# A graph network in three edge passes: how far GpSimd may gather ahead of the sums

## The chip, the cores and the metric

One NeuronCore of a Trainium2 chip runs the kernel, with its five engines: TensorE (PE in the profile, PEld for its weight loads), VectorE (DVE), ScalarE (ACT), GpSimd (POOL) and SyncE (SP). The metric is the time of one execution on the device in microseconds (us), as the median of several runs.

## The reference

A graph of 6250 nodes with 128 features and 100000 edges, sorted by destination, so each node's incoming edges stand in a row. Two layers work on it, each added to its input and normalised over the features:

```
x = layernorm(x + sigmoid(gcn(relu(gcn(x, W1, b1)), W2, b2)))      # both gcn over the same edges
x = layernorm(x + attention(x, edge_attr, fc_w, fc_r_w, attn_w, loop_w))

gcn(x, W, b)    h = x W;  out[d] = sum over edges (s, d) of h[s] * dinv[s] * w * dinv[d], plus b
                dinv = 1/sqrt(sum of the edge weights into a node, and 1 for its own loop)
attention       z = x fc_w^T;  r = edge_attr fc_r_w^T
                e = leakyrelu(z[s].a0 + z[d].a1 + r.a2);  alpha = softmax of e over the edges into d
                out[d] = relu(sum of alpha * (z[s] + r), plus z loop_w)
```

## The kernel before, in words

**Tiles and groups.** Edges go by tiles of 128 (T = 782), tiles by groups of eight (G = 98). For each tile the kernel needs the feature rows of its 128 source nodes. GpSimd fetches them with one indirect DMA for a tile (L720), at an offset column of `srcC`, into a slot of `ring` in SBUF. VectorE makes for each tile a 128 x 128 matrix S (`build_S`, L1608), which holds an edge's weight at the column of its destination within a window, and TensorE multiplies the gathered rows by S into a PSUM bank that collects the window's nodes (`sum_group`, L858). A node bank is closed when its last group is in: ScalarE copies it out, TensorE applies the layer's weights, and so on.

**Three passes.** Pass 0 and pass 1 are the two gcn layers, pass 2 is the attention. A pass begins its gathers when the table it reads (`x1_d`, `h1_d`, `x2_d`) has been written whole. Nine sets of 32 tiles need no gather in some passes: their rows come from a node table in SBUF by one-hot matmuls (`look_up`, L898, with one-hots that ScalarE makes at L1239 and L1241) and are summed in slots (`make_slots`, L1681 on VectorE; `sum_slots`, L910 on TensorE). In pass 0 six sets are so made, in pass 1 all nine, in pass 2 three (`XR`). So the gathered groups are 74, 62 and 86 (`GL[0]`, `GL[1]`, `GATHERED`), 590, 494 and 686 tiles, 1770 gathers in all. Pass 2 has three far chunks, the groups 38 to 41, 62 to 65 and 86 to 89, which have no gathers; their far rows come by L1020, L1033 and L1045. But each group of them still has its own eight matmuls with the edge attributes (L860).

**Pass 2's softmax.** It goes by chunks of four groups (`CH`: 0 and 1, then 2 to 5, 6 to 9 and so on; the last four have two). Before VectorE can build the S of chunk c, it needs the chunk's attention weights: `scores(c)` adds a gathered column to the edges' own terms (L1917, L1920), TensorE turns it (`turn_e`, L995), VectorE takes maxima along a node's edges (L1963 to L1965), ScalarE the exponent (L1352), VectorE sums and divides (L1970 to L1973), TensorE turns it back (`turn_alpha`, L1001), VectorE copies (L1978). A node's edges may lie across the border of a chunk, so `scores(c)` reads the chunk's rows and the first tile of the next chunk, unless that one is far. In TensorE's order the turn of e of chunk c stands ahead of the sums of the last group before it, and the turn of alpha behind them.

**Orders and queues.** Each engine runs one list of instructions, written out by hand, and waits on semaphores. On GpSimd's list there are, besides a few constants, only the gathers: in a pass, group after group, eight tiles each. Ahead of a group's gathers stand the group's waits (L709 to L715). `summed` counts groups whose sums are done, over all passes (`AT` holds the count at which each pass begins), so `summed >= gg - R + 1` lets group gg into the slot of group gg - 18. Passes 0 and 1 have R = 18 ring slots, pass 2 R2 = 12, since it keeps other tiles in the remaining six. Each single gather also waits until the gather six before it has landed (`LANES`). S has four slots (NS), so VectorE builds at most four groups ahead of the sums.

**Prologue.** Before pass 0, the index columns are made: `src`, `dst` and the weights are loaded in rows, turned by TensorE and copied by VectorE (`cols_copied` counts seven copies: first source columns, two of ranks, two of weights, two of the remaining source columns, L1513). Then the degrees: for each of 98 groups VectorE or ScalarE (three to one) makes one-hots in bf16 (L1571, L1191), TensorE sums them (L811), and `deg_summed` counts the groups. After the search for odd columns (`find_odd`) in between, `setup_done` frees a part of the ring that the setup used; group 9's gathers wait for it. With the degrees, x is scaled and stored as `x1_d`. The gathers of pass 0's first 18 groups (R0) need none of that: they read the input x, and the factor goes into S later. They are issued in the prologue. From group 18 on they wait for `x1_stored`.

Of the kernel before, what the change touches and what calls it, by code (L numbers as in the profile page):

```python
# [28 lines left out]
R = 18  # L29
R0 = 18  # L30
NS = 4
NR = 8
ND = 16
NJ = 6
R2 = 12
NQ2 = 7
# [15 lines left out]
def tiles(q):  # L52
    return range(q * GT, min((q + 1) * GT, T))
# [60 lines left out]
AT = [0, HS[0], HS[0] + HS[1]]  # L114
# [75 lines left out]
GATHERED = [q for q in range(G) if q not in FAR_SETS]  # L190
# [47 lines left out]
def build(nc, x, src, dst, edge_attr, edge_weight, W1, b1, W2, b2, fc_w, fc_r_w, attn_w, loop_w, out):  # L238
    ctx = ExitStack()
    with ctx:  # L240
# [41 lines left out]
        S, rh = SR[:, 0:NS], SR[:, NS:NS + NR]  # L282
        SH = SR[:, 0:ND // 2].rearrange("p s t w -> p (s t w)").bitcast(BF16).rearrange("p (s t w) -> p s t w", s=ND, t=GT)
        Z = rh.rearrange("p s t w -> p (s t w)")
# [41 lines left out]
        pre = preX[:, :, :, 0:D]  # L326
        junk = U[:, 0:NJ * P].rearrange("p (a d) -> p a d", d=P)
        dloP = Z[:, 3 * GT * W:(3 + NP_DLO) * GT * W].bitcast(BF16).rearrange("p (a g n) -> p a g n", a=NP_DLO, g=2)
# [90 lines left out]
        def s(name):  # L419
            if name not in sems:  # L420
                sems[name] = sem(name)
            return sems[name]
# [41 lines left out]
        def ecols(g):  # L464
            return bass.ds(g * GT, GT)
# [228 lines left out]
        @block.gpsimd  # L694
        def _(pool):
            nc.gpsimd.memset(srcR[:, EB - 1, :], 0).then_inc(s("pads_set"), 1)
            nc.gpsimd.memset(dstR[:, EB - 1, :], int(FAR)).then_inc(s("pads_set"), 1)
            nc.gpsimd.memset(ewR[:, EB - 1, :], 0.0).then_inc(s("pads_set"), 1)
            nc.gpsimd.iota(iota_i, [[1, NARROW]], base=0, channel_multiplier=0).then_inc(s("iota_made"), 1)
            nc.gpsimd.iota(pidx_i[:, :], [[1, 1]], base=0, channel_multiplier=1).then_inc(s("iota_made"), 1)  # L700
            nc.gpsimd.memset(rows[:, NB - 1, 0:D], 0.0).then_inc(s("pads_set"), 1)
            nc.gpsimd.iota(baseI, [[GT, TC]], base=-MARGIN, channel_multiplier=0).then_inc(s("iota_made"), 1)

            def gathers(p, table, width):
                for h, q in enumerate(GL[p] if p < 2 else GATHERED):
                    gg = AT[p] + h
                    if p == 0 and h == R0:
                        pool.wait_ge(s("x1_stored"), 16 * 7)
                    if p == 0 and h == R - 9:  # L709
                        pool.wait_ge(s("setup_done"), 1)  # L710
                        pool.wait_ge(s("dpad_stored"), 64)
                    if p == 2 and h >= R2:
                        pool.wait_ge(s("summed"), AT[2] + GATHERED[h - R2] + 1)
                    elif p < 2 and gg >= R:
                        pool.wait_ge(s("summed"), gg - R + 1)  # L715
                    for k, t in enumerate(tiles(q)):
                        i = turn(p, t)
                        if i >= LANES:
                            pool.wait_ge(landed[i % LANES], 16 * (i // LANES))
                        pool.indirect_dma_start(ring[:, ring_at(p, h if p < 2 else q), k, 0:width], None, (x if p == 0 and h < R0 else table)[:, :],  # L720
                                                bass.IndirectOffsetOnAxis(ap=srcC[:, t:t + 1], axis=0)).then_inc(landed[i % LANES], 16)
                    if p == 0 and h == P // GT - 1:
                        pool.wait_ge(s("cols_copied"), 7)

            pool.wait_ge(s("cols_copied"), 1)
            gathers(0, x1_d, D)
            pool.wait_ge(*stored(h1_stored, NA - 2))
            pool.wait_ge(*stored(h1_stored, NA - 1))
            gathers(1, h1_d, D)
            pool.wait_ge(*stored(x2_stored, NA - 2))  # L730
            pool.wait_ge(*stored(x2_stored, NA - 1))
            gathers(2, x2_d, XW)

            def wide_gathers(n, phase, table, width, stored):
                pool.wait_ge(stored, 16)
                with pool.Fori(0, G) as g:
                    pool.wait_ge(s("wide_group"), g + (phase * G + 1))
                    pool.sem_inc(s("pool_passed"))
                    nc.gpsimd.tensor_copy(stageW, srcC[:, ecols(g)]).then_inc(s("wide_staged"), 1)
                    pool.wait_ge(s("wide_staged"), g + (n * G + 1))  # L740
                    pool.sem_inc(s("pool_passed"))
                    for k in range(GT):
                        pool.indirect_dma_start(wring[:, k, 0:width], None, table[:, :],
                                                bass.IndirectOffsetOnAxis(ap=stageW[:, k:k + 1], axis=0)).then_inc(s("wide_gathered"), 16)

            with any_wide(pool):
                pool.wait_ge(s("out_stored"), 16 * NA)
                nc.gpsimd.iota(baseWi, [[GT, TC]], base=-MARGIN, channel_multiplier=0).then_inc(s("wide_iota"), 1)
                wide_gathers(0, 1, x1_d, D, s("wide_x1_stored"))
                wide_gathers(1, 2, h1_d, D, s("wide_h1_stored"))  # L750
                wide_gathers(2, 3, x2_d, XW, s("wide_x2_stored"))
                wide_gathers(3, 4, x2_d, D, s("wide_x2_stored"))

        @block.tensor
        def _(pe):
# [44 lines left out]
            for q in range(G):  # L800
# [4 lines left out]
                for j, t in enumerate(tiles(q)):  # L805
                    for k, lo, hi, w0 in pieces(t):
                        if t == FIRST[k]:
                            if k >= 2:
                                pe.wait_ge(s("deg_evac"), k - 1)
                            clear(ps[6 + k % 2][0:3, :], 3)  # L810
                        last = nc.tensor.matmul(ps[6 + k % 2][0:3, lo:hi], ewP[:, t, :], SH[:, q % ND, j, w0:w0 + hi - lo],  # L811
                                                start=False, stop=t == LAST[k])
# [363 lines left out]
        def _(act):  # L1176
# [7 lines left out]
            for i, q in enumerate(DEG_ACT):  # L1184
                for k in range(NK):
                    if q - 4 < CLOSE[k] + 3 <= q:
                        evacuate_deg(k)
                if q >= ND:
                    act.wait_ge(s("deg_summed"), q - ND + 1)
                for j, t in enumerate(tiles(q)):  # L1190
                    last = nc.scalar.activation(SH[:, q % ND, j, :], iota_h[:, :], ACT.Abs, bias=rankC[:, t:t + 1], scale=-1.0)  # L1191
                last.then_inc(s("deg_onehot_act"), 1)
                act.wait_ge(s("deg_onehot_act"), 2 * i + 1)
                n = len(tiles(q))
                nc.scalar.activation(SH[:, q % ND, 0:n, :], SH[:, q % ND, 0:n, :], ACT.Relu, bias=ones[:, 0:1], scale=-1.0).then_inc(s("deg_onehot_act"), 1)
            for k in range(NK):
# [267 lines left out]
        def _(dve):  # L1464
# [240 lines left out]
            def dot(attr, t):  # L1705
                n = dots[0]
                if n >= NJ:
                    dve.wait_ge(s("rh_dotted"), n - NJ + 1)
                v.scalar_tensor_tensor(junk[:, n % NJ, :], attr, 1.0, v2B[:, :], ALU.mult, ALU.mult, accum_out=s2C[:, t:t + 1]).then_inc(s("rh_dotted"), 1)  # L1709
                dots[0] = dotted[t] = n + 1  # L1710
# [549 lines left out]
```

## Time and profile before

| | us |
|---|---|
| median of 3 timed runs | 2408.18 |
| lowest and highest of them | 2407.04, 2409.39 |
| span of the profiled execution | 3348.6 |
| busy in it: PE, PEld | 2044.2, 1762.3 |
| busy in it: DVE, ACT, POOL | 1834.8, 946.7, 1718.9 |
| mean granted TensorE clock in it | 0.787 of full speed |

The profiled execution is the only one with a trace, and it took 940 us more than the timed ones; every duration below is from it. POOL's 1718.9 us are 1770 gathers of about 0.97 us each. A row of the timeline has the start in us from the span's start, the duration, engine, line, operation and tiles; in brackets the time its engine was idle before it and what ended that: an instruction of another engine, a DMA, "issue" if it waited for nothing the profile shows, "remote" if the release came from something the profile can't name. A row of stretches has the stretch, its length, then the busy us of PE, PEld, DVE, ACT and POOL with the number of instructions, the granted clock, the DMA engines' share and GB/s.

### The profile page before, as it was taken

The page shows a single profiled execution, that of the slowest core. Times are in us where ns is not written, and L with a number is a line of the kernel's source. Part 1 is how long each engine was busy: PE and PEld are TensorE (multiplying, and loading weights), DVE is VectorE, ACT ScalarE, POOL GpSimd, SP SyncE. Part 2 cuts the span into 40 slices and gives each one's busy share as a digit, 9 for nine tenths or more (in the row PEclk, how much of TensorE's full clock was granted, in tenths as well). Part 3 has the DMA queues.
Part 4 walks back from the last instruction along what each step waited for, and adds up shares of the span by engine and source line. Part 5 has one row for each costly group of instructions (what it writes and reads, how often), then busy time and mean ns, then how long its engine had stood idle before and what let it go on. Part 6 is the DMA issues. An engine that isn't in the chain of part 4 may idle for free.

```text
span 3348.6 us, 40819 instructions
## 1 busy us (share of the span) xinstructions
PE 2044.2 (61%) x13384; PEld 1762.3 (53%) x13384; DVE 1834.8 (55%) x7005; ACT 946.7 (28%) x1754; POOL 1718.9 (51%) x1781
## 2 busy tenths in 40 slices
PE   1416444588888911177777888106677667756786
PEld 1315433566767811166666677005666666645675
DVE  3626435577779810156656687217654564546457
ACT  1316000122233300033333444101254225412541
POOL 7351666665550067466556500555766646663640
PEclk9857667798999955588988899557778778877888
DMA  4112221222221122123333332525343534443431
GB/s 118 30 42 66 69 61 47 61 61 63 60 62 32 51 76 53 41 74 86 99 103 102 93 91 80 138 62 147 97 103 97 134 93 102 108 117 79 103 97 34
DMA packets 272093, 270.54 MB, mean 81 GB/s; under 512 B 43454, under 2 KB 218709, under 8 KB 271862
## 3 DMA queue, kind: packets, MB, share of 16 engines
q1 hardware_dynamic: 201790, 143.87, 15.1%
q0 software_dynamic: 56640, 117.52, 14.8%
q10 hardware_dynamic: 13448, 6.47, 0.7%
q8 instruction: 112, 1.84, 0.2%
q14 instruction: 103, 0.84, 0.1%
HBM read 254.14 MB, written 13.97 MB: 80 GB/s over the span
## 4 chain that ended last, share of the span: by engine, by line
PE 35%; DVE 21%; another core or an unknown queue 21%; issue 15%; ACT 4%; SPq 1%; DMA 1%; POOL 1%; ACTq 0%; DVEq 0%; POOLq 0%
PE ps L858 9%; PE ps L910 8%; DVE SR L1608 5%; PE ps L860 3%; PE ps L898 3%; PE ps L1045 2%; DVE U L1709 2%; DVE SR L1681 2%; DVE SR L1571 1%; PE ps L885 1%; DVE U L1648 1%; PE ps L1029 1%; POOL ring L720 1%; PE ps L792 1%
## 5 line engine op out<-in xcount | busy, mean ns | idle before, releaser
L720 POOL DMA_INDIRECT ring<-x_d,srcC x1132 | 1109.7, 980 | 971.2 <-issue 579.0
L858 PE MATMUL ps<-SR,ring 128*128 128x128 f32 x3540 | 672.5, 320 | 205.0 <-issue 132.0
L858 PEld LDWEIGHTS ps<-SR,ring 128*128 128x128 f32 x3540 | 580.5, 231 | 238.9 <-issue 178.9
L720 POOL DMA_INDIRECT ring<-h_d,srcC x494 | 469.9, 951 | 457.1 <-DMA h_d<-Lb 170.9
L1681 DVE TENSOR_SCALAR SR<-iota_r,cols 128x288 f32<-128x288 f32 x735 | 365.0, 564 | 303.9 <-remote 226.6
L910 PE MATMUL ps<-SR 128*128 128x288 f32 x1470 | 416.6, 435 | 118.1 <-ACT SR L1232 75.3
L910 PEld LDWEIGHTS ps<-SR 128*128 128x128 f32 x1470 | 292.3, 205 | 212.7 <-ACT SR L1232 77.5
L860 PE MATMUL ps<-SR 128*128 128x128 f32 x1564 | 340.3, 312 | 40.8 <-issue 34.6
L1232 ACT COPY SR<-ps 128x512 f32<-128x512 f32 (+1 forms) x195 | 106.0, 561 | 758.4 <-remote 502.9
L860 PEld LDWEIGHTS ps<-SR 128*128 128x128 f32 x1564 | 279.6, 228 | 48.3 <-issue 48.0
L898 PE MATMUL ps<-rows,SR 128*128 128x128 f32 x1470 | 196.2, 285 | 122.5 <-ACT SR L1241 90.6
L898 PEld LDWEIGHTS ps<-rows,SR 128*128 128x128 f32 x1470 | 186.7, 200 | 134.0 <-ACT SR L1241 96.0
L1608 DVE TENSOR_SCALAR SR<-iota,rankC,ewC 128x128 f32<-128x128 f32 x940 | 253.3, 357 | 2.6 <-DVE U L1812 1.1
L1608 DVE TENSOR_SCALAR SR<-iota,rankC,cols 128x128 f32<-128x128 f32 x782 | 213.0, 355 | 14.7 <-issue 11.7
L720 POOL DMA_INDIRECT ring<-in_x_dram,srcC x144 | 137.3, 953 | 93.7 <-issue 90.5
L1571 DVE TENSOR_SCALAR SR<-iota_h,rankC 128x128 bf16<-128x128 bf16 x584 | 107.6, 260 | 125.9 <-issue 106.1
L1709 DVE SCALAR_TENSOR_TENSOR U<-SR,v2B 128x128 f32<-128x128 f32 x686 | 156.0, 286 | 34.3 <-DVE U L1709 18.1
L1239 ACT ACTIVATE SR<-SR,negp 128x512 bf16<-128x512 bf16 (+1 forms) x195 | 134.9, 692 | 112.0 <-remote 100.3
L811 PE MATMUL ps<-SR,cols 128*3 128x128 bf16 (+2 forms) x974 | 74.0, 237 | 110.7 <-issue 57.0
L1241 ACT ACTIVATE SR<-SR,negp 128x512 f32<-128x512 bf16 (+1 forms) x195 | 135.9, 697 | 6.4
L1963 DVE TENSOR_TENSOR_SCAN U<-U,ps 32x384 f32<-32x384 f32 (+2 forms) x27 | 25.4, 942 | 203.8 <-remote 115.7
L811 PEld LDWEIGHTS ps<-SR,cols 128*3 128x3 bf16 x974 | 60.0, 96 | 123.5 <-issue 65.0
(288 smaller groups left out, 2703.4 us busy)
## 6 DMA issues: line engine op xcount, KB each, us to landing
SR<-in_edge_attr_dram SPq DMA_DIRECT2D x97, 512.0 KB
SR<-low_d SPq DMA_DIRECT2D x90, 256.0 KB
U<-dlo_d SPq DMA_DIRECT2D x74, 256.0 KB
ring<-x_d,srcC POOLq DMA_INDIRECT x1132
ring<-h_d,srcC POOLq DMA_INDIRECT x494
SR<-dlo_d SPq DMA_DIRECT2D x12, 512.0 KB
ring<-in_edge_attr_dram SPq DMA_DIRECT2D x12, 512.0 KB
U<-lo_d SPq DMA_DIRECT2D x18, 256.0 KB
```

Source lines behind the costliest of these rows:

```text
L720: pool.indirect_dma_start(ring[:, ring_at(p, h if p < 2 else q), k, 0:width], None, (x if p == 0 and h < R0 else table)[:, :], bass.Indire ...
L811: last = nc.tensor.matmul(ps[6 + k % 2][0:3, lo:hi], ewP[:, t, :], SH[:, q % ND, j, w0:w0 + hi - lo], start=False, stop=t == LAST[k])
L858: last = nc.tensor.matmul(ps[(p * NA + k) % 2][:, at], ring[:, ring_at(p, h), j, 0:D], S[:, gg % NS, j, :], start=False, stop=stop)
L860: last = nc.tensor.matmul(ps[2 + k % 2][:, at], rh[:, q % NR, j, :], S[:, gg % NS, j, :], start=False, stop=stop)
L898: last = nc.tensor.matmul(ps[3 + m % 2][:, i * P:(i + 1) * P], ohS[:, m % 2, i * P:(i + 1) * P], rows[:, a, 0:D], start=True, stop=True)
L910: nc.tensor.matmul(ps[5][:, SLACK:SPAN], rowX[:, m % 2, i * P:(i + 1) * P], slotS[:, n % NQ, :], start=False, stop=a == NB - 1).then_inc(s ...
L1239: nc.scalar.activation(low, low, ACT.Abs, bias=negp[:, 0:1]).then_inc(s("low_apart"), 1)
L1241: return nc.scalar.activation(out, low, ACT.Relu, bias=negp[:, 1:2], scale=-1.0)
L1571: last = v.tensor_scalar(SH[:, q % ND, j, :], iota_h[:, :], rankC[:, t:t + 1], None, ALU.is_equal)
L1608: last = v.tensor_scalar(S[:, gg % NS, j, :], iota[:, :], rankC[:, t:t + 1], w[:, t:t + 1], ALU.is_equal, ALU.mult)
L1681: v.tensor_scalar(slotS[:, n % NQ, :], iota_up, slotD[:, RUNS[i], a:a + 1], slotW[:, RUNS[i], a:a + 1], ALU.is_equal, ALU.mult).then_inc(s ...
L1709: v.scalar_tensor_tensor(junk[:, n % NJ, :], attr, 1.0, v2B[:, :], ALU.mult, ALU.mult, accum_out=s2C[:, t:t + 1]).then_inc(s("rh_dotted"), 1)
```

## The change

In passes 1 and 2 the gathers of group h wait until the sums of the sixth gathered group before it are done (LEAD = 6), where they waited for the eighteenth before it in pass 1 and the twelfth in pass 2. The first six groups of a pass are free of it, as before. In pass 0 the rule for group 18 and later stays. Of the eighteen early groups, 2 to 5 now wait for copied columns (3, 5, 7 and 7 copies), and group h from 6 to 17 waits for 6(h - 5) degree sums: 6 for group 6, 72 for group 17. The tiles, the slots and the list of gathers stay the same.

```diff
--- before.py
+++ after.py
@@ -31,6 +31,7 @@
 NS = 4
 NR = 8
 ND = 16
+LEAD = 6
 NJ = 6
 R2 = 12
 NQ2 = 7
@@ -709,10 +710,16 @@
                     if p == 0 and h == R - 9:
                         pool.wait_ge(s("setup_done"), 1)
                         pool.wait_ge(s("dpad_stored"), 64)
-                    if p == 2 and h >= R2:
-                        pool.wait_ge(s("summed"), AT[2] + GATHERED[h - R2] + 1)
-                    elif p < 2 and gg >= R:
+                    if p == 2 and h >= LEAD:
+                        pool.wait_ge(s("summed"), AT[2] + GATHERED[h - LEAD] + 1)
+                    elif p == 1 and h >= LEAD:
+                        pool.wait_ge(s("summed"), gg - LEAD + 1)
+                    elif p == 0 and gg >= R:
                         pool.wait_ge(s("summed"), gg - R + 1)
+                    elif p == 0 and 2 <= h < 6:
+                        pool.wait_ge(s("cols_copied"), 2 * h - 1 if h < 5 else 7)
+                    elif p == 0 and 6 <= h:
+                        pool.wait_ge(s("deg_summed"), 6 * (h - 5))
                     for k, t in enumerate(tiles(q)):
                         i = turn(p, t)
                         if i >= LANES:
```

## Rows read from the trace of the kernel before

**Rows 1.** Page of the kernel before: its span.

```profile
span 3348.6 us, 40819 instructions
```

**Rows 2.** Chain that ended last, whole span: shares by line.

```profile
by line: another core or an unknown queue 21.2%; issue 15.5%; PE ps L858 8.8%; PE ps L910 8.2%; DVE SR L1608 4.9%; PE ps L860 3.0%; PE ps L898 3.0%; PE ps L1045 2.0%; DVE U L1709 1.8%; DVE SR L1681 1.7%; DVE SR L1571 1.3%; PE ps L885 1.2%; 
```

**Rows 3.** Stretches: length, busy us of PE, PEld, DVE, ACT, POOL, clock, DMA, GB/s.

```profile
0.00:316.00 316.00, 108.08 (x1204) 88.23 (x1205) 147.18 (x711) 102.30 (x260) 139.27 (x155) 0.78 0.24 62
...
1180.00:1413.00 233.00, 34.98 (x121) 26.05 (x121) 16.53 (x47) 8.53 (x13) 158.29 (x168) 0.53 0.22 56
1413.00:2117.00 704.00, 545.16 (x3496) 462.13 (x3496) 464.88 (x1553) 276.41 (x433) 311.30 (x326) 0.89 0.35 95
2117.00:2273.00 156.00, 11.27 (x205) 7.79 (x202) 33.56 (x150) 0.52 (x1) 90.97 (x96) 0.50 0.37 93
2273.00:3349.00 1076.00, 742.98 (x4492) 663.59 (x4492) 617.94 (x2836) 386.45 (x732) 582.07 (x590) 0.79 0.39 99
```

**Rows 4.** Chain that ended last, window 1180 to 1413 us, shares by line.

```profile
by line: another core or an unknown queue 92.8%; DVE SR L1681 4.3%; DVE SR L1608 2.7%; issue 0.1%; DVE odd L1564 0.1%; DVE flag L1565 0.1%
```

**Rows 5.** Timeline (start, duration us, engine, line; in brackets the idle before), VectorE.

```profile
1218.57 0.37 PE L898 MATMUL ps<-rows,SR 128*128 128x128 f32 x1 [2.43 <-issue]
...
1387.98 0.57 DVE L1681 TENSOR_SCALAR SR<-iota_r,cols 128x288 f32<-128x288 f32 x1 [194.92 <-remote]
```

**Rows 6.** DMA queues and issues, window 1200 to 1390 us.

```profile
q0 software_dynamic: 4864, 9.97, 20.8%
...
ring<-h_d,srcC POOLq DMA_INDIRECT x152
```

**Rows 7.** Timeline of VectorE, prologue.

```profile
54.84 0.25 DVE L1571 TENSOR_SCALAR SR<-iota_h,rankC 128x128 bf16<-128x128 bf16 x1 [1.15 <-issue]
...
107.34 22.52 DVE L1571 TENSOR_SCALAR SR<-iota_h,rankC 128x128 bf16<-128x128 bf16 x138 [0.45 <-issue]
```

**Rows 8.** Timeline of GpSimd, prologue.

```profile
143.87 0.97 POOL L720 DMA_INDIRECT ring<-in_x_dram,srcC  x1 [47.25 <-issue]
```

**Rows 9.** Timeline of GpSimd, start of pass 1.

```profile
1187.25 0.94 POOL L720 DMA_INDIRECT ring<-h_d,srcC  x1 [0.30 <-issue]
1188.50 0.94 POOL L720 DMA_INDIRECT ring<-h_d,srcC  x1 [0.30 <-issue]
```

**Rows 10.** Timeline of VectorE, prologue: copies of the source columns.

```profile
21.64 0.91 DVE L1513 CAST srcC<-ps 128x512 int32<-128x512 f32 x2
```

**Rows 11.** Timeline of PE, sums of groups 54 and 61, pass 1.

```profile
2039.96 1.27 PE L858 MATMUL ps<-SR,ring 128*128 128x128 f32 x9 [1.98 <-DVE SR L1608]
...
2096.04 1.50 PE L858 MATMUL ps<-SR,ring 128*128 128x128 f32 x12
```

**Rows 12.** Timeline, chunk of groups 34 to 37 in pass 2, VectorE and PE.

```profile
2657.47 0.27 DVE L1917 TENSOR_TENSOR cols<-ring,s1C 128x15 f32<-128x15 f32 x2
...
2665.67 0.51 PE L995 MATMUL ps<-ident,cols 128*32 128x128 f32 x3
...
2674.38 2.14 DVE L1608 TENSOR_SCALAR SR<-iota,rankC,cols 128x128 f32<-128x128 f32 x8
...
2676.62 0.77 PE L858 MATMUL ps<-SR,ring 128*128 128x128 f32 x2 [3.39 <-issue]
```

**Rows 13.** Timeline of PE, a group's sums in pass 2, first and last.

```profile
2862.49 0.39 PE L858 MATMUL ps<-SR,ring 128*128 128x128 f32 x2
...
2865.84 0.39 PE L860 MATMUL ps<-SR 128*128 128x128 f32 x2
```

**Rows 14.** Timeline of PE, turns of e of the four last chunks.

```profile
3269.69 0.49 PE L995 MATMUL ps<-ident,cols 128*16 128x128 f32 x3
...
3319.08 0.49 PE L995 MATMUL ps<-ident,cols 128*14 128x128 f32 x3
```

**Rows 15.** Timeline of GpSimd, first far chunk of pass 2.

```profile
2763.19 0.94 POOL L720 DMA_INDIRECT ring<-x_d,srcC  x1 [28.94 <-PE ps L860]
```

**Rows 16.** Timeline of PE, first sum of pass 1 opens its bank.

```profile
1191.21 0.58 PE L792 MATMUL ps<-iota_r,zero_h 1*128 1x512 bf16 x1 [15.69 <-DMA ring<-h_d,srcC]
```

## The prediction

> **What bounds the kernel now.** I began with the times against the page: the timed runs have a median of 2408.18 us, the profiled execution has a span of 3348.6 us [rows 1]. So 940 us of the recorded execution are in no timed run, and before any row is costed the reader must know which stretches they fill. The chain of waits gives the answer: 21.2% of it is released by nothing the profile shows and 15.5% is "issue" [rows 2], together 36.7% or 1229 us. Of those at least a part is real (a semaphore's way, a fetch), but 1229 is the only item large enough to hold 940.
>
> Next, where this idle time lies. The busy time by stretch [rows 3] has two stretches in which PE, DVE and ACT nearly stand still while GpSimd gathers at its full rate: 1180 to 1413 us, the start of pass 1 (PE 35 of 233 us, DVE 17, POOL 158), and 2117 to 2273, the start of pass 2 (PE 11 of 156, POOL 91). In the first, 92.8% of the chain is released by nothing visible [rows 4]. In the timeline a matmul of the block lookup waits 2.43 us for "issue", and VectorE sits 194.92 us before L1681 [rows 5]. Between 1200 and 1390 us the gathers' queue carries 9.97 MB, and 152 gathers are all that the program issued [rows 6], so no load is late. The prologue shows it most simply: the one-hots of L1571 wait on nothing inside a group, yet at 54.84 us each starts 1.40 us after the one before, while gathers run; from 107.34 us, with GpSimd idle (it starts again only at 143.87), 138 of them take 22.52 us, 0.163 us each [rows 7, 8]. Every engine crawls once gathers have run without a pause, one instruction at a time and the same on all.
>
> I take this crawl for a cost of recording. Reason: it is proportional to instructions and descriptors and not to work, and its total fits the 940 us that the timed runs lack. The Trainium skill has a rule that fits: "NOTIFIC — the notification-queue block", section 7.1, says that the block's internal pipeline holds producers back rather than lose a record. No row here shows such a queue; by that rule the crawl would be gone from the timed runs, which is the case my sum takes anyway.
>
> Taking the crawl out, what is left is the gather rate. Inside a run of gathers they start 1.25 us apart (0.94 busy, 0.30 issue) [rows 9], crawl or not. Pass 2 has 86 gathered groups, 686 gathers, 858 us; pass 1 494 gathers, 618 us; pass 0 another 446 after x1 is stored, 558 us. That makes 2034 us; with some 190 us until x1 is stored (VectorE's 147 us of work in the first stretch [rows 3] and, my estimate, 40 for loads, dinv and the store), and 40 us for the last softmax, sums and normalising, plus 20 to 30 us for the two turns between passes, it is 2290. 2408 is 118 above it: GpSimd is the bound or close to it for most of the run, and PE and DVE are not far behind (PE 743 us busy of 1076 in pass 2, part of it crawl) [rows 3].
>
> **The change part by part.** The edit adds no work and removes none: the same 1770 gathers, one wait more in front of some groups. Only gathers stand behind a wait on GpSimd, so what is delayed is ring rows, and who waits for them: PE's sums (L858) and in pass 2 VectorE's scores (L1917).
>
> (1) Prologue, groups 2 to 5 wait for copied columns. The last of these copies run from 21.64 us on [rows 10]; group 2 is reached after 16 gathers, 20 us at 1.25, and group 4, which needs the last copy, after 40. Cost 0.
>
> (2) Prologue, group h from 6 waits for 6(h-5) degree sums. Without crawl a degree group of VectorE is 8 x 0.163 = 1.3 us, and three in four are its own, so one ends per 1.0 us; they are under way at 54.84 us even recorded [rows 7]. From 50 us, with 10 more allowed for the search of odd columns in between, sum 6 is there at 56 and sum 72 at 132 us. Group 6 is reached after 48 gathers, 60 us, group 17 after 136, 170 us. Never late: cost 0 in the timed runs. In the recorded execution the same waits do bind, since 1.40 us instructions are what delays the sums: there gathers and degree sums will take turns, and the recorded prologue gets shorter. If that crawl were in the timed runs it would be a gain; see the rivals.
>
> (3) Pass 1, group h waits for sum h-6 in place of h-18. GpSimd needs 10 us a group. As long as sums are slower than that, six groups (60 us) ahead is as good as eighteen; where they are quicker, GpSimd never gets six ahead. Only a change from slow to quick can use up the cover. The end of the pass is one: first sums 2039.96 (group 54) to 2096.04 (group 61), 8.0 us a group [rows 11], which eats 7 x 2 = 14 of 60 us. Cost 0, at most 5.
>
> (4) Pass 2, the same with the index in the gathered list, in place of 12. Here it matters, for two reasons. First, scores(c) reads rows up to the first tile of the next chunk: for chunk C..C+3 that is a tile of group C+4, whose gathers may now begin only after sum C-2. Second, a far chunk (38 to 41, 62 to 65, 86 to 89) has four groups of PE and DVE work and no gathers, in which GpSimd could bank up to twelve groups, and now six.
>
> The chunk's clock: GpSimd 4 x 10 = 40 us. From the turn of e (2665.67) to the first sum of the chunk (2676.62) is 11 us [rows 12], of which PE fills some 4 with sum C-1 (a group's 32 matmuls take 3.6 us at full pace [rows 13]). PE's own work is 743/98 = 7.6 us a group with crawl and slow clock in it, and 4492 x 0.11/98 = 5.0 at full pace [rows 3, 13]; a chunk is 4 x 5.0 to 4 x 7.6, plus 7, that is 27 to 37 us. GpSimd's 40 is the longer. Within a gathered chunk the new wait then hardly binds: with scores at T, sum C ends at T+16, sum C+1 at T+23, C+2 at T+30, and GpSimd reaches C+6, C+7, C+8 at T+16.5, T+26.5, T+36.5. Cost 0 to 1 us.
>
> At a far chunk it binds. When the sum of the group before it ends, GpSimd has some four groups in hand and may gather two more, 20 us; then it stands until the first group behind the far chunk is summed: 20 to 30 us of PE work, 11 of chain, 4 of sum, so 36 to 45. It idles 16 to 25 us at each of three. Before, with twelve allowed, it could go on for six groups more. The bank was worth 40 less the sums' period for each chunk that followed: 3 us (PE at 37) to 16 and more. At 3, the five chunks up to the next far one use 15; at the third the turns of e of the four two-group chunks are 16.5 us apart (3269.69 to 3319.08 in three steps) against GpSimd's 20 [rows 14], so up to 14 comes due. I take 14 + 14 + 10 = 38 us, the slow-PE end, since PE's recorded time is the nearest row; the quick end is 25 + 25 + 14 = 64. If the gather without recording takes nearer to its busy 0.94 us (30 us a chunk) [rows 9], the sums are the bound and the price falls towards 0 to 5. The recorded row agrees with the mechanism: GpSimd idled 28.94 us at the first far chunk even with twelve allowed [rows 15].
>
> Sum: 0 + 0 + 0 + 38: on the median 2408 + 38 = 2446 us. The steps are made from the gather's spacing and counts, which the recorded execution's extra 940 us do not touch; the recorded span itself should fall, and says nothing of the median.
>
> The Trainium skill has one rule that could change the gather price: "SBUF — State Buffer", section "SBUF: two separate sides", says in its box on the "DVE blocks DMA" trap GpSimd can't write descriptors while VectorE holds the shared port. Here gathers keep 0.94 us beside a busy VectorE at their median, and a later, thinner gather stream meets no less VectorE work, so I leave the sum as it is.
>
> **Rivals.** (A) The crawl is real in the timed runs too. At most 1229 - 940 = 289 us of it, 24%, can be. Then the short bursts pay: at the start of pass 1, 168 gathers ran for 210 us [rows 3, 9] and would now stop after 60, 150 us of crawl less; 60 less at pass 2 (12 groups to 6); in the prologue some 80 of the 316 - 190 = 126: 24% of 290 is 70 us. Against it some of (4), 5 to 38: 2345 to 2375 us, middle 2370. For it: the sheer pattern. Against it: the 940.
> (B) Sums bound pass 2, gathers have room: nothing moves, 2408 (2404 to 2412). It needs a gather under some 1.1 us, or PE over 37 us a chunk, and scores not made late.
> (C) Sums bound, and the scores are made late, on the slow side. A gathered tile is there 0.94 + 1.77 us after its issue begins (the last tile of group 0 of pass 1 is issued at 1188.50, done at 1189.44, and PE goes on at 1191.21 [rows 9, 16]); so scores come 2.7 us or more after sum C-2 at each of some 19 chunks, where now VectorE scores at 2657.47 and the turn at 2665.67 waits for PE alone [rows 12]. 19 x (2.7 + 0.5) = 60 us: 2468. It decides only where PE has no slack in the chunk, that is if PE's period is above 40 us.
>
> **How the numbers follow.** Forecast (GpSimd bound, far chunks) 0.45, own range 2413 to 2472; C 0.13; B 0.22; A 0.20. A measurement tells about 0.2% (5 us) from no change. Slower by more: 0.45 + 0.13 = 0.58; within: 0.22; faster: 0.20. Range for 8 in 10: the top takes in C with some spread, 2480; the bottom half of A, 2365.
>
> **What the profile after would show.** Right if: GpSimd waits for L860 or L858 of some 20 us or more at groups behind 41, 65 and 89, and the recorded burst at the start of pass 1 is 48 gathers; the recorded span falls by 200 us or so while the median rises. In the prologue GpSimd waits for L811. Wrong if the median falls along with the recorded span (A), or if VectorE waits for gathers at L1917 in nearly every chunk while GpSimd idles (C). What would upset all of it is a gather that costs something else without recording.

## The result, and the profile after

| | before | changed |
|---|---|---|
| median, us | 2407.61 (4 runs, 2403.52 to 2409.39) | 2459.82 (4 runs, 2455.35 to 2470.11) |
| ratio, 95% interval | | 1.0228 [1.0208, 1.0249] |
| span of the profiled execution | 3348.6 | 2457.9 |

The change costs 52 us by the two medians and 55 by the ratio; its interval, 50 to 60 us, holds both. The recorded span of the changed kernel is that of its timed runs, so this recording has nothing of the slow crawl that filled 940 us of the first one [rows 1 to 5].

All lines of the changed kernel are seven higher: the gathers are L727, the sums L865 and L867, the scores L1924. First its page: the span, busy time by engine, and the chain that ended last.

```profile
span 2457.9 us, 40834 instructions
...
PE 1851.8 (75%) x13384; PEld 1640.5 (67%) x13384; DVE 1816.8 (74%) x7005; ACT 946.3 (39%) x1754; POOL 1744.1 (71%) x1781
...
POOL 28%; DVE 26%; PE 24%; issue 14%; DMA 5%; ACT 2%; SPq 2%; ACTq 0%; POOLq 0%; DVEq 0%
POOL ring L727 27%; PE ps L865 7%; PE ps L917 6%; DVE SR L1615 5%; DVE SR L1578 4%; PE ps L905 2%; DMA ring<-x_d,srcC 2%; PE ps L892 2%; DVE SR L1688 2%; PE ps L867 2%; DVE U L1655 2%; DVE U L1716 1%; PE ps L879 1%; DMA ring<-in_edge_attr_dram 1%; PE ps L799 1%
```

Where "an unknown queue" led the chain with 21.2% [rows 2], the gathers now do with 27%; most of this difference is the crawl's, since in the second recording of the kernel before, below, the gathers have 24%. The waits of the changed kernel, whole span (engine, tile and line that waited, what released it, then us in total, times, longest), have what is new:

```profile
DVE cols L1924 <- DMA ring<-x_d,srcC: 234.2, 18, 19.7
...
POOL ring L727 <- PE ps L867: 65.6, 11, 28.1
```

GpSimd stands still for the sums of pass 2, 65.6 us in 11 waits. Three of them have most of it. The timeline of GpSimd at the groups 48, 72 and 96 (start, duration, the idle time before in brackets):

```profile
1933.82 0.94 POOL L727 DMA_INDIRECT ring<-x_d,srcC  x1 [0.30 <-issue]
1948.35 0.97 POOL L727 DMA_INDIRECT ring<-x_d,srcC  x1 [13.58 <-PE ps L867]
...
2161.88 0.96 POOL L727 DMA_INDIRECT ring<-x_d,srcC  x1 [0.30 <-issue]
2190.90 0.94 POOL L727 DMA_INDIRECT ring<-x_d,srcC  x1 [28.06 <-PE ps L867]
...
2393.11 0.94 POOL L727 DMA_INDIRECT ring<-x_d,srcC  x1 [0.30 <-issue]
2401.87 0.94 POOL L727 DMA_INDIRECT ring<-x_d,srcC  x1 [7.82 <-PE ps L867]
```

Each of the three is a group whose sixth gathered group before is the first behind a far chunk (42, 66, 90). The others are short: before 14 (1.5 us), 29 (3.8), 53 (3.5) and 69 (5.2). In the passes 0 and 1 and in the prologue GpSimd never waits for a sum or a degree group longer than the 0.3 us that stand between any two gathers.

### The profile page after: what moved, and what is told of

It reads as the page before. It is cut to its first block, busy times and chain, and to the rows that moved or that the text cites. A ratio compares the mean times of both kernels' runs of the same rounds, so it can differ in the third digit from the quotient of the medians.

```text
span 2457.9 us, 40834 instructions
## 1 busy us (share of the span) xinstructions
PE 1851.8 (75%) x13384; PEld 1640.5 (67%) x13384; DVE 1816.8 (74%) x7005; ACT 946.3 (39%) x1754; POOL 1744.1 (71%) x1781
## 4 chain that ended last, share of the span: by engine, by line
POOL 28%; DVE 26%; PE 24%; issue 14%; DMA 5%; ACT 2%; SPq 2%; ACTq 0%; POOLq 0%; DVEq 0%
POOL ring L727 27%; PE ps L865 7%; PE ps L917 6%; DVE SR L1615 5%; DVE SR L1578 4%; PE ps L905 2%; DMA ring<-x_d,srcC 2%; PE ps L892 2%; DVE SR L1688 2%; PE ps L867 2%; DVE U L1655 2%; DVE U L1716 1%; PE ps L879 1%; DMA ring<-in_edge_attr_dram 1%; PE ps L799 1%
## 5 line engine op out<-in xcount | busy, mean ns | idle before, releaser
L727 POOL DMA_INDIRECT ring<-x_d,srcC x1132 | 1120.5, 990 | 431.9 <-issue 355.0
L865 PE MATMUL ps<-SR,ring 128*128 128x128 f32 x3540 | 629.9, 311 | 98.8 <-DVE SR L1615 53.7
L865 PEld LDWEIGHTS ps<-SR,ring 128*128 128x128 f32 x3540 | 554.3, 225 | 124.0 <-issue 63.0
L727 POOL DMA_INDIRECT ring<-h_d,srcC x494 | 475.8, 963 | 196.9 <-issue 193.4
L917 PE MATMUL ps<-SR 128*128 128x288 f32 x1470 | 378.4, 410 | 0.0
L867 PE MATMUL ps<-SR 128*128 128x128 f32 x1564 | 329.8, 307 | 6.0 <-DVE SR L1615 6.0
L917 PEld LDWEIGHTS ps<-SR 128*128 128x128 f32 x1470 | 274.7, 193 | 70.9 <-issue 2.8
L867 PEld LDWEIGHTS ps<-SR 128*128 128x128 f32 x1564 | 273.1, 224 | 6.3 <-issue 6.1
L727 POOL DMA_INDIRECT ring<-in_x_dram,srcC x144 | 145.8, 1012 | 46.8 <-issue 40.5
L1924 DVE TENSOR_TENSOR cols<-ring,s1C 128x32 f32<-128x32 f32 (+6 forms) x31 | 5.3, 190 | 234.5 <-DMA ring<-x_d,srcC 234.2
L1716 DVE SCALAR_TENSOR_TENSOR U<-SR,v2B 128x128 f32<-128x128 f32 x686 | 152.2, 288 | 6.0 <-DMA SR<-in_edge_attr_dram 4.4
L1002 PE MATMUL ps<-ident,cols 128*32 128x128 f32 (+2 forms) x81 | 20.5, 386 | 177.5 <-DVE cols L1927 161.0
L1002 PEld LDWEIGHTS ps<-ident,cols 128*32 128x32 f32 (+2 forms) x81 | 7.1, 115 | 184.7 <-DVE cols L1927 166.2
L1359 ACT ACTIVATE U<-U 32x384 f32<-32x384 f32 (+2 forms) x27 | 14.1, 523 | 271.2 <-DVE U L1972 271.2
```

The lines of the kernel that those rows point to most:

```text
L865: last = nc.tensor.matmul(ps[(p * NA + k) % 2][:, at], ring[:, ring_at(p, h), j, 0:D], S[:, gg % NS, j, :], start=False, stop=stop)
L867: last = nc.tensor.matmul(ps[2 + k % 2][:, at], rh[:, q % NR, j, :], S[:, gg % NS, j, :], start=False, stop=stop)
L917: nc.tensor.matmul(ps[5][:, SLACK:SPAN], rowX[:, m % 2, i * P:(i + 1) * P], slotS[:, n % NQ, :], start=False, stop=a == NB - 1).then_inc(s ...
```

## The experiments

Eleven edits of the kernel before, and that kernel itself once more, were each timed in turns with it on the same chip, in three sets in which the kernel before had 2405.84, 2406.45 and 2407.69 us. A cost in us is the ratio less one, times 2407.

### The kernel before, recorded again

No edit. 

> The kernel before, unchanged, profiled once more. If the crawl of the first recorded execution belongs to that recording, this one has a span near 2405 us, no stretch in which VectorE's one-hots come 1.40 us apart, and GpSimd without long idle times in pass 2. If the crawl belongs to the kernel (gathers far ahead of the sums), the span is again well over 2408, some 3300 us.

Measured: 2407.43 us, ratio 1.0001 [0.9991, 1.0011]. Its page:

```profile
span 2409.0 us, 40819 instructions
...
PE 1836.9 (76%) x13384; PEld 1624.6 (67%) x13384; DVE 1817.0 (75%) x7005; ACT 946.7 (39%) x1754; POOL 1747.9 (73%) x1781
```

The same program with a span of 2409.0 in place of 3348.6 [rows 1]: the crawl came from that one recording, and none of it is in a timed run. From here on the durations of before are this trace's. Three readings of it matter below. First VectorE's waits in pass 2 at the scores, and GpSimd's in the whole span:

```profile
DVE cols L1917 <- DMA ring<-x_d,srcC: 148.1, 14, 20.1
```

```profile
POOL ring L720 <- issue: 583.4, 1691, 43.6
...
POOL ring L720 <- PE ps L858: 1.5, 5, 0.3
```

With twelve or eighteen groups allowed GpSimd never waits for a sum longer than the 0.3 us between two gathers. Second, the end of pass 0:

```profile
776.84 1.10 POOL L720 DMA_INDIRECT ring<-x_d,srcC  x1 [0.30 <-issue]
821.54 0.95 POOL L720 DMA_INDIRECT ring<-h_d,srcC  x1 [43.59 <-issue]
822.79 0.94 POOL L720 DMA_INDIRECT ring<-h_d,srcC  x1 [0.30 <-issue]
```

The gathers of pass 0 are done 43.59 us before those of pass 1 can begin. Third, how many groups are gathered and not yet summed when a group's first gather starts, counted from the two timelines: at most 14 in pass 0, 2 in pass 1, and in pass 2 five or six mostly, rising to 7 behind the first far chunk and 9 behind the second. A limit of n can bind only where this count reaches n.

### One part of the change at a time

The kernel before with the edit of one pass alone:

```diff
-                    if p == 2 and h >= R2:
-                        pool.wait_ge(s("summed"), AT[2] + GATHERED[h - R2] + 1)
+                    if p == 2 and h >= 6:
+                        pool.wait_ge(s("summed"), AT[2] + GATHERED[h - 6] + 1)
```

> Six ahead in pass 2 alone; passes 0 and 1 as before. Theory (GpSimd bound, the price falls due behind the far chunks of pass 2): nearly the whole price, 2450 to 2460 us. If pass 1 or the prologue carried a part of it, it would be 2410 to 2440.

Pass 1 alone:

```diff
-                    elif p < 2 and gg >= R:
+                    elif p == 1 and h >= 6:
+                        pool.wait_ge(s("summed"), gg - 6 + 1)
+                    elif p == 0 and gg >= R:
                         pool.wait_ge(s("summed"), gg - R + 1)
```

> Six ahead in pass 1 alone. Theory: the cover of 60 us is not used up, 2405 to 2413 us. Rival (lead lost at the quick end of the pass): 2415 to 2430.

The prologue alone:

```diff
+                    elif p == 0 and 2 <= h < 6:
+                        pool.wait_ge(s("cols_copied"), 2 * h - 1 if h < 5 else 7)
+                    elif p == 0 and 6 <= h:
+                        pool.wait_ge(s("deg_summed"), 6 * (h - 5))
```

> Only the waits of the early gathers for copied columns and degree sums. Theory: none binds, 2405 to 2411 us. Rival (the waits hold up gathers that pass 0 needs, or thin a stream that disturbs the degree sums): outside that, either way, 10 us or more.

| part | median, us | ratio, 95% interval |
|---|---|---|
| pass 2 | 2458.28 | 1.0213 [1.0199, 1.0227] |
| pass 1 | 2406.51 | 0.9999 [0.9989, 1.0009] |
| prologue | 2406.78 | 0.9999 [0.9990, 1.0008] |

Pass 2 alone costs 51 us by its ratio, which is the whole price within the intervals. Pass 1 can't feel a limit of six, since GpSimd is there never more than two ahead.

### Seven and nine groups in pass 2

The edit of pass 2 above with 9, then with 7 for 6.

> The kernel before with nine groups ahead in pass 2 instead of twelve. In its own trace GpSimd is at no start of a gathered group of pass 2 more than nine groups ahead of the sums, and nine only once. Theory (what counts is how many groups GpSimd banks over a far chunk): nine binds at most once, by less than a group's 10 us: 2407 to 2411 us, the same as before. Rival (each step down costs its share, 52 us / 6 = 9 us a group): 2430 us or more.

> Seven groups ahead in pass 2. Six costs 51 us. Theory (each far chunk loses a whole group's gathers, 10 us, for each group that may not be banked, less what the sums wait for anyway): one group more at each of three far chunks gives back 20 to 30 us: 2428 to 2440 us. Rival (the price lies in the first tile of the next chunk, whose gathers begin two groups ahead of the scores under six and three ahead under seven): nearly all of it comes back, 2408 to 2415 us.

Measured: nine 2405.15 us, ratio 0.999 [0.998, 1.0]; seven 2432.01 us, 1.0105 [1.0088, 1.0121]. So nine costs nothing, seven costs 25 us and six another 26. With nine, GpSimd's waits for the sums are the first line below, with seven the second (L720 and L860 are the gathers and the sums):

```profile
POOL ring L720 <- PE ps L860: 4.3, 2, 4.0
```

```profile
POOL ring L720 <- PE ps L860: 28.5, 4, 23.0
```

The price begins below the counted bank of nine, and not at each step from twelve down; eight was not run, so whether it begins there or at seven stays open. Nor do these runs say which groups carry it.

### The groups around the far chunks: one choice that missed, one that hit

First the groups 42 to 47, 66 to 71 and 90 to 95 were freed of the limit, and then they alone bound:

```diff
+def lead_of(h):
+
+    spans_far = h >= 6 and GATHERED[h] - GATHERED[h - 6] > 6
+    return R2 if spans_far else 6
...
-                    if p == 2 and h >= R2:
-                        pool.wait_ge(s("summed"), AT[2] + GATHERED[h - R2] + 1)
+                    if p == 2 and h >= lead_of(h):
+                        pool.wait_ge(s("summed"), AT[2] + GATHERED[h - lead_of(h)] + 1)
```

> The kernel before, with the wait of pass 2 at six groups back, except for the groups 42 to 47, 66 to 71 and 90 to 95, whose six-back group stands across a far chunk: these keep twelve. Theory (the price is that of the three far chunks, where GpSimd may no longer bank): the idle time at 48, 72 and 96, 13.6 + 28.1 + 7.8 = 49.5 us in the changed kernel's trace, goes, and what is left is the ones at 14, 29, 53 and 69 (1.5 + 3.8 + 3.5 + 5.2 = 14 us), of which part is made good later: 2408 to 2420 us. Rival (any gathered group late by a little in each chunk, scores made late all along): the far groups are 18 of 86, most of the price stays, 2440 to 2460 us.

With `return 6 if spans_far else R2`:

> The other half: the kernel before with twelve ahead as it was, and six only for the groups 42 to 47, 66 to 71 and 90 to 95 of pass 2. Theory of the far chunks: 35 to 50 us over the kernel before, 2442 to 2458 us; GpSimd idle 10 to 35 us before 48 and 72. Since no other group is held, GpSimd can win some back between two far chunks by running up to twelve ahead: so rather the lower end. Rival (late scores in every chunk): 0 to 15 us, 2407 to 2422.

Measured: freed 2458.59 us, 1.0223 [1.0203, 1.0243]; bound 2406.30 us, 1.0001 [0.9992, 1.0011]. Taken by the numbers alone, both speak for the rival: the far chunks would carry nothing. The trace says that the question was put to the wrong groups. With those groups freed, GpSimd still stands before group 48, 15.34 us where the changed kernel has 13.58:

```profile
1929.33 0.94 POOL L727 DMA_INDIRECT ring<-x_d,srcC  x1 [0.31 <-issue]
1945.61 0.94 POOL L727 DMA_INDIRECT ring<-x_d,srcC  x1 [15.34 <-PE ps L867]
```

The sixth gathered group before 42 is 32, before 47 it is 37: all of them ahead of the far chunk, and summed before GpSimd arrives. Behind the second far chunk one isn't: in the run that bound these groups alone GpSimd waits 5.1 us before 69, and the time doesn't show it. The first group whose sixth before stands behind the far chunk is 48. So the edit moved waits that cost nothing in either form, and what it shows is only that. The theory still had to be tried, with the choice by the traced waits (the two lines of the wait use `lead_of` as above):

```diff
+def lead_of(h):
+    return 6 if GATHERED[h] in (48, 72, 96) else R2
```

> The kernel before, with six groups ahead only in front of three groups of pass 2: 48, 72 and 96, whose sixth gathered group before is the first behind a far chunk (42, 66, 90). These are the places where the changed kernel's trace shows GpSimd idle for 13.6, 28.1 and 7.8 us. Theory (the price is the bank of gathered groups that a far chunk used to build): most of it comes with these three waits alone, 30 to 50 us over the kernel before: 2437 to 2456 us, with GpSimd idle 10 to 40 us before 48 and 72. Rival (the price is made of small delays in every chunk, and the idle time there is only where it comes to light): 2407 to 2420 us.

and its counterpart:

```diff
+def lead_of(h):
+    return R2 if GATHERED[h] in (*range(48, 60), *range(72, 84), 96, 97) else 6
```

> The counterpart: six groups ahead in pass 2 except for the groups behind a far chunk, 48 to 59, 72 to 83, 96 and 97, which keep twelve (26 of 86 groups). Theory of the bank: most of the 52 us is given back, 2408 to 2422 us; what idle time is left is that before 14, 29 and 69 (1.5 to 5 us each), and GpSimd is up to seven to nine groups ahead behind the far chunks. Rival (small delays all along): 2435 us or more.

Measured: three waits alone 2449.79 us, 1.0178 [1.0164, 1.0193], so 43 us; all but the groups behind far chunks 2415.50 us, 1.0034 [1.0022, 1.0046], so 8 us. The two together are 51, as the whole of pass 2. GpSimd with three waits:

```profile
1941.12 0.94 POOL L725 DMA_INDIRECT ring<-x_d,srcC  x1 [15.41 <-PE ps L865]
...
2181.43 0.98 POOL L725 DMA_INDIRECT ring<-x_d,srcC  x1 [34.66 <-PE ps L865]
...
2391.94 0.94 POOL L725 DMA_INDIRECT ring<-x_d,srcC  x1 [7.81 <-PE ps L865]
```

GpSimd idles 57.9 us at three places, and the time rises by 43. Three waits of 686 gathers make five sixths of the price. In the counterpart GpSimd is again seven ahead behind the first far chunk and eight behind the second, and its longest wait for a sum is 6.12 us.

### Is GpSimd the bound? Its own work, added to one pass

The kernel before, with four small settings of a spare tile on GpSimd ahead of each group, one after the other (the declarations of the tile and of the counter `spared` are left out here):

```diff
+                    for k in range(4 if p == 2 else 0):
+                        nc.gpsimd.memset(spare[:, :], 0.0).then_inc(s("iota_made"), 1)
+                        spared[0] += 1
+                        pool.wait_ge(s("iota_made"), spared[0])
                     for k, t in enumerate(tiles(q)):
```

> The kernel before, with four small settings of a spare 128x16 tile on GpSimd ahead of each of the 86 gathered groups of pass 2, each waiting for the one before it. Their cost is to be read in the run's own trace; from the 0.20 us of a 128x128 setting and 0.12 of a 128x1 one, my estimate is 0.15 to 0.3 us each, 0.6 to 1.2 us a group, 50 to 100 us in all. If GpSimd's gathers bound pass 2, as the prediction says, the time rises by most of that sum, less what the bank at the far chunks hides: 60 to 100 per cent of it. If the sums bound it (rival B), by under 10 us.

The same for the groups of pass 0 from 18 on (`if p == 0 and h >= R0`):

> The same work ahead of each of the 56 groups of pass 0 that are gathered after x1 is stored (34 to 67 us in all). In pass 0 GpSimd is done some 40 us before the sums (its last gather at 775, the next pass's first at 821.5 in the second recording of the kernel before), so the sums bound it: 0 to 10 us, 2406 to 2417, as long as the added work stays under those 40 us. If GpSimd bounds pass 0 too, as the prediction's count of 2290 us of gathers took it, the whole 34 to 67 us appear.

What a group's work costs, from the timeline of GpSimd in the run of pass 2:

```profile
1708.16 0.95 POOL L727 DMA_INDIRECT ring<-x_d,srcC  x1 [0.30 <-issue]
1709.11 0.64 POOL L720 MEMSET spare<- 128x16 f32 x4
1710.34 0.95 POOL L727 DMA_INDIRECT ring<-x_d,srcC  x1 [0.59 <-POOL spare L720]
```

From the end of the last gather (1709.11) to the next one are 1.23 us where 0.30 stood: 0.93 us a group, 80 us for 86 groups. Measured in pass 2: 2479.59 us, 1.0304 [1.0290, 1.0318], that is 73 us, nine tenths of what was added. So GpSimd bounds pass 2 as a whole.

The prediction let the gathers keep 0.94 us beside a busy VectorE. Their median does; single ones don't. Of the 1770 in the second recording of the kernel before 220 took over 1.0 us, 88 of them in pass 2. The longest began within a VectorE operation and ended behind it:

```profile
1588.86 1.90 DVE L1936 TENSOR_TENSOR ring<-iota,ring 128x1666 bf16<-128x1666 f32 x1
1589.12 2.45 POOL L720 DMA_INDIRECT ring<-x_d,srcC  x1 [0.30 <-issue]
```

It goes by the operation: of the 39 gathers that overlap L1650, which takes two tiles, 36 took over 1.0 us, and of the 25 that overlap the softmax's sum L1971 24, but of the 532 beside the S of L1608 only 60. In pass 2 all this adds 29 us over the median, and 29 in the changed kernel too, so it is no part of the price. The "DVE blocks DMA" box of the Trainium skill's page "SBUF — State Buffer" says that during a VectorE operation in a two-port mode GpSimd is locked out of the shared port and can't write descriptors. The long gathers look like that, but no row shows the port or the mode, and no run here took such an operation away.

In pass 0 the same work gave 2428.34 us, 1.0083 [1.0069, 1.0096]: 20 us of at least 56 x 0.93 = 52. The end of pass 0 in this run:

```profile
834.69 0.95 POOL L727 DMA_INDIRECT ring<-x_d,srcC  x1 [0.30 <-issue]
842.97 0.95 POOL L727 DMA_INDIRECT ring<-h_d,srcC  x1 [7.33 <-issue]
```

The last gather moved from 776.84 to 834.69, by 57.9 us, and the idle time behind it fell from 43.59 to 7.33, by 36.3. The other 21 us moved pass 1. I had expected up to 10 us as long as the work stayed under 40; it was 58, and the slack is 36. So pass 0 is bound by its sums, with GpSimd some 36 us from being the bound: neither of the two answers written down before was the whole one.

## Why the prediction was right, point by point

**The crawl is a cost of recording.** Right, and shown: the same program was recorded without it, 2409.0 us of span. The rival A (2370 us) has nothing left to stand on. The Trainium skill's page "NOTIFIC — the notification-queue block", section 7.1, says that the block's pipeline holds producers back rather than lose a record. That the timed runs lack the 940 us fits it; but the second recording lacks them too, no row shows the queue, and why one recording crawled and the next did not stays open.

**What bounds.** GpSimd in pass 2, as said, at 1.25 us a gather: shown by the added work, with the stretches behind the far chunks as exceptions (below). The first two gathers of pass 1, before which nothing is in flight, are 1.25 us apart too (821.54 and 822.79 in the kernel before, recorded again), so it is the gather's own spacing. But pass 0 is bound by its sums: the sum of 2290 us took 446 gathers of pass 0 as the bound, and some 60 of its missing 118 us lie ahead of pass 1, whose first gather comes at 821.54 where 190 + 558 and a turn make some 760. Another 31 are in pass 2: its 686 gathers take 889 us in place of 858, nearly all of it by the long ones above. Neither had weight in the forecast, since the edit left pass 0's rule alone and the long gathers are in both kernels.

**Steps 1 and 2, the prologue.** Cost 0, as measured. The side remark, that in a recording the gathers and the degree sums would take turns and GpSimd would wait for L811, wasn't borne out: with no crawl in the recording, the waits for degree sums never held a gather. Whether they would have under a crawl stays open. For the same reason the 48 gathers at the start of pass 1 and the fall of the recorded span by 200 us were not there to be seen: the span fell by 891, and all of it is the recording's.

**Step 3, pass 1.** Cost 0, measured. The reason given counted a cover of 60 us against a tail of 14. There is no such cover: GpSimd is at most two groups ahead there, and the limit is never reached.

**Step 4, within a gathered chunk.** I gave 0 to 1 us. Everything but the groups behind far chunks costs 8 us. In the changed trace it is 1.5 us before group 14 and 3.8 before 29, seen whole in the scores that follow, and in the counterpart another 5.2 before group 69 and 6.12 before group 84, where the bank of the freed groups meets the limit again.

**Step 4, the far chunks.** This is the term that carried the forecast, and the wait is the one described: GpSimd gathers on through the far chunk up to its limit and stands until the first group behind it is summed. The idle times forecast were 16 to 25 us at each; the trace has 13.58, 28.06 and 7.82, none of them within. What each cost is read from the scores, which open every chunk. VectorE's scores of the chunks from 42, 46, 50, 66, 70, 82 and 90 on, first the kernel before as recorded again:

```profile
1927.80 0.21 DVE L1917 TENSOR_TENSOR cols<-ring,s1C 128x32 f32<-128x32 f32 x1
...
1953.84 0.21 DVE L1917 TENSOR_TENSOR cols<-ring,s1C 128x32 f32<-128x32 f32 x1 [2.74 <-DMA ring<-x_d,srcC]
...
1995.46 0.28 DVE L1917 TENSOR_TENSOR cols<-ring,s1C 128x15 f32<-128x15 f32 x2 [9.22 <-DMA ring<-x_d,srcC]
...
2153.85 0.27 DVE L1917 TENSOR_TENSOR cols<-ring,s1C 128x15 f32<-128x15 f32 x2
2177.72 0.21 DVE L1917 TENSOR_TENSOR cols<-ring,s1C 128x32 f32<-128x32 f32 x1
...
2281.62 0.21 DVE L1917 TENSOR_TENSOR cols<-ring,s1C 128x31 f32<-128x31 f32 x1 [6.38 <-DMA ring<-x_d,srcC]
2329.58 0.18 DVE L1917 TENSOR_TENSOR cols<-ring,s1C 128x16 f32<-128x16 f32 x1
```

and the changed kernel:

```profile
1932.24 0.21 DVE L1924 TENSOR_TENSOR cols<-ring,s1C 128x32 f32<-128x32 f32 x1
...
1971.07 0.21 DVE L1924 TENSOR_TENSOR cols<-ring,s1C 128x32 f32<-128x32 f32 x1 [15.46 <-DMA ring<-x_d,srcC]
...
2015.40 0.27 DVE L1924 TENSOR_TENSOR cols<-ring,s1C 128x15 f32<-128x15 f32 x2 [18.09 <-DMA ring<-x_d,srcC]
...
2174.76 0.27 DVE L1924 TENSOR_TENSOR cols<-ring,s1C 128x15 f32<-128x15 f32 x2
2213.53 0.21 DVE L1924 TENSOR_TENSOR cols<-ring,s1C 128x32 f32<-128x32 f32 x1 [15.49 <-DMA ring<-x_d,srcC]
...
2334.30 0.21 DVE L1924 TENSOR_TENSOR cols<-ring,s1C 128x31 f32<-128x31 f32 x1 [17.00 <-DMA ring<-x_d,srcC]
2379.23 0.19 DVE L1924 TENSOR_TENSOR cols<-ring,s1C 128x16 f32<-128x16 f32 x1
```

| stretch | before, us | changed, us | cost | forecast |
|---|---|---|---|---|
| chunk 42 to chunk 50, behind the first far chunk | 67.7 | 83.2 | 15.5 | 14 |
| chunk 66 to chunk 82, behind the second | 127.8 | 159.5 | 31.8 | 14 |
| chunk 82 to chunk 90, over the third | 48.0 | 44.9 | -3.0 | 10, behind it |

With the 4.4 us that the changed kernel is already behind at chunk 42, this is 48.7 of the 49 us between the two spans. So the first term came out in size, the second was mis-sized by 18 us, and the third should have been nothing. That the first came out is luck: forecast were 3 us in each of five chunks, but the bank pays 12.8 us in the first chunk (26.0 us before, 38.8 changed), 2.7 in the second, and from chunk 50 to 66 one us in 159.

The second failed at one number: "at 3, the five chunks up to the next far one use 15". The 3 us were 40 less a period of the sums of 37, the slow end, taken from a recording with a crawl in it. (The "16 and more" beside it doesn't follow from the prediction's own quick end either: 40 less 27 is 13.) The true period is (2281.62 - 2177.72) / 3 = 34.6 us while the bank lasts. The changed kernel runs these three chunks in (2334.30 - 2213.53) / 3 = 40.3 us, GpSimd's pace. The bank there is worth 5.6 us a chunk, and another 38.8 less 23.9 = 15 us in the first chunk alone, whose rows lay ready in the ring. The busy time by stretch shows who sets the 34.6 (columns as in [rows 3]; first before, chunks 66 to 82, then changed):

```profile
2154.00:2282.00 128.00, 112.29 (x802) 102.29 (x803) 91.95 (x447) 84.47 (x165) 97.51 (x101) 0.93 0.53 135
```

```profile
2175.00:2334.00 159.00, 122.08 (x829) 111.29 (x829) 90.96 (x443) 89.03 (x174) 108.48 (x113) 0.85 0.46 116
```

Before, PE is busy 112 of 128 us: with rows in hand the sums run at nearly its full pace. Changed, it is busy 122 of 159.

Why does the second far chunk cost twice the first? Its stretch is longer, and a bank grows with it. From the last sum before the far chunk to the first behind it PE takes 28 us at the first (1915 to 1943) and 44 at the second (2142 to 2186). The changed kernel in these two:

```profile
1915.00:1943.00 28.00, 23.16 (x164) 20.22 (x163) 21.19 (x101) 17.67 (x40) 15.19 (x16) 0.87 0.58 158
2142.00:2186.00 44.00, 19.95 (x121) 17.78 (x120) 40.65 (x165) 11.69 (x24) 16.88 (x14) 0.76 0.33 90
```

In the second VectorE is busy 40.65 of 44 us, while PE has work for 20. By its busy share VectorE sets this length, with the S of the far groups, the edges' own terms (46 of L1716 where the first has 27) and the maxima of two chunks where the first has one. It also has four operations on 128x1568 or 128x1666 numbers, L1943 to L1957, of 1.8 to 1.9 us each, of which the first stretch has none. No run took one of these away, so this cause is read from the trace and not tested. I had put "20 to 30 us of PE work" and eleven of chain on all three alike; for the second neither the engine nor the sum was right. Behind the third far chunk only eight groups are left, in chunks of two that the sums pace in both kernels, so GpSimd's 7.82 us before group 96 cost nothing at the end.

So 38 us were forecast, and 15.5 + 31.8 - 3.0 + 4.4 = 48.7 us stand in the traces. That 2446 lies 14 us from the measured 2459.82 owes something to luck: 18 us too few at the second far chunk stand against 13 too many at the third. The quick-end bound of 64 us held the truth between the ends, and the choice of the slow end rested on durations that the prediction itself had called cost of recording.

**The rivals.** B (the sums bound pass 2, 2408 us) is excluded by the 73 us that the added work costs. C (scores late in every chunk, 2468 us) is nearest by the time and wrong by its mechanism: it wants a loss in some 19 chunks, and freeing 26 groups behind far chunks takes 44 of 52 us away. Its sign, VectorE waiting for gathers at the scores, is in both kernels (148.1 us in 14 waits before, 234.2 in 18 changed): so the sign alone tells nothing; GpSimd's own waits must stand beside it.

**What stays open.** The short waits at 14 and 29 were not taken apart, eight groups ahead were not run, and why the second far stretch is the longer and what lengthens the long gathers are read from traces alone. Why the changed kernel is 3 us quicker over the third far chunk wasn't looked into. No version was faster than the kernel before: nine groups gave 0.999 [0.998, 1.0], no difference.

## What to carry to other kernels

A limit on how far an engine may run ahead costs nothing where that engine never gets far ahead (two groups at most in pass 1), and nothing down to the highest count of items in hand that the trace shows (nine here). Further down it takes away what is banked over stretches that need nothing of the bounding engine, so size the limit by the longest such stretch. Price it by how fast the consumer runs on a full buffer, not by its mean pace, and look at each stretch for itself: two that look the same in the code were 28 and 44 us long. And choose the instructions of an experiment by the waits in the trace, not by a rule on indices: two runs went to groups that stood next to the right ones.

## What the runs showed of the hardware

One recording of a program had a span of 3348.6 us and the next one of the same program 2409.0, with timed runs of 2407 to 2408 beside both: a recording has to be held against the timed runs before a duration is taken from it. The indirect gather of 128 rows took 0.94 to 0.95 us and 1.25 from start to start, as the median of every pass in both kernels. 220 of 1770 took over 1.0 us and up to 2.45, nearly all that overlap certain VectorE operations (36 of 39 at L1650). TensorE's granted clock, a mean of its two levels of 1.2 and 2.4 GHz, was 0.93 of full speed in the chunks 66 to 82 of the kernel before, and 0.85 in the same chunks of the changed one, where PE stood idle for 37 us in place of 16. Its matmuls there (802 and 829 recorded) took 122 us in place of 112; since a chunk then goes by GpSimd's pace of 40.3 us, I count none of the ten us to the price, but no run separates the two.
